# Second attention of a two-layer vision tower: the moving average's products and adds placed in its first iterations

## The chip, the cores and the metric

One core of a Trainium2 chip runs the whole program. The metric is device time in microseconds (us) of that core. TensorE, VectorE, ScalarE and GpSimd are called PE, DVE, ACT and POOL in the profile.

## What is computed

64 images become 65 tokens of 128 channels each; two layers follow, each with an attention and experts, and a normalisation after each of the four. The part that matters is the third normalisation's input: an attention and a moving average over the same `x`, blended by two weights.

```python
def _L1_attn_ref(x, ...):
    ...
    dots = jnp.einsum('bhid,bhjd->bhij', q, k) * dk ** (-0.5)
    ...
    dots = dots * mask.astype(dots.dtype)
    attn = jax.nn.softmax(dots, axis=-1)
    out_attn = jnp.einsum('bhij,bhjd->bhid', attn, v)
    out_attn = out_attn.transpose(0, 2, 1, 3).reshape(b, n, e) @ W_out + b_out
    def step(h, xt):
        h = p_coeff[None] * xt[:, :, None] + q_coeff[None] * h
        return (h, jnp.sum(gamma[None] * h, axis=-1))
    h0 = jnp.zeros((b, e, ndim), x.dtype)
    _, ys = jax.lax.scan(step, h0, jnp.swapaxes(x, 0, 1))
    x_cema = jnp.swapaxes(ys, 0, 1)
    w = jax.nn.softmax(adaptive_weights)
    return w[0] * out_attn + w[1] * x_cema

h = _L0_tok_ref(...)
h = _layernorm(h + _L0_attn_ref(h, ...), axis=-1)
h = _layernorm(h + _L0_ffn_ref(h, ...), axis=-1)
h = _layernorm(h + _L1_attn_ref(h, ...), axis=-1)
h = _layernorm(h + _L1_ffn_ref(h, ...), axis=-1)
```

## The kernel before, in words

Everything is float32. The 64 images are worked on in 16 groups of 4 (260 token columns). `vision_tower` (L1907) calls the stages one after the other; each is a block with one hand-written list per engine, and between two blocks all engines meet. In order: `embed_and_attend`, `route_and_gather`, `run_experts`, `scatter_and_norm`, `moving_average`, `attend_causally`, `norm_and_route`.

`scatter_and_norm` (L1127) adds the experts' outputs `yout` to the tokens and normalises; it leaves the result twice: by feature in `h_feat` (what projections read) and by token in `h_tok`. GpSimd puts `h_tok` plus a bias into `base`. A transfer on SyncE brings `lags` meanwhile: for each of the 128 channels a 65x65 matrix that turns the recurrence of the reference into one product over tokens.

`moving_average` (L1282) multiplies channel by channel: 16 chunks of 8 channels, each chunk filling one bank of 512 columns (64 images by 8 channels), four banks in turn. TensorE (L1302) signals `done` per chunk, VectorE (L1310) adds the bank, times the blend's weight, to `base` and signals `added`; TensorE needs `added` of four chunks back.

`attend_causally` (L1315) is a software pipeline over groups. `pipeline` (L97) runs an engine's loop with a lead: its variable g starts at -2 or -1, and one pass works on several groups, so that group g + 2 is projected and group g + 1 scored while group g is finished. The first and the last passes are written out; a hardware loop runs the middle. Per group:

- TensorE projects queries and keys (L1380, L1381) into the bank group `b_scores`. ScalarE copies queries into `qm` (L1558), which waits before its first pass for `v_cleared`, and keys into `kt` (L1561). GpSimd builds `qlast` for the last token (L1647) and copies the group's features to `b_h` (L1640).
- TensorE makes scores (L1372, L1375). VectorE masks them into `e` (L1478), finds the peaks and subtracts them (L1484 to L1497). ScalarE takes exponents (L1550), VectorE sums and inverts (L1503, L1505), GpSimd multiplies (L1655).
- TensorE makes values (L1386), ScalarE copies them to `vs` (L1582). TensorE turns the weights (L1400 to L1413), ScalarE copies them to `at` (L1570), TensorE multiplies by the values (L276), ScalarE copies to `ot`, TensorE applies the output weights (L1395), and VectorE adds `base` into `z` (L1513).

The scores of group g + 1 wait until the values of group g are out of `b_scores`. Before its first pass GpSimd clears `vs` twice and half of `at` (L1664, L1666); VectorE makes `parity_bias` (L1523) and, after a product with `mean` (L1432), `gate` (L1525); TensorE waits for that `gate` before its first pass.

## Time and profile before

| | |
|---|---|
| median of 3 runs | 704.71 us (704.68 to 706.1) |
| profiled execution | 712.94 us, its span 711.0 us |
| PE busy | 575.1 us, 81% |
| DVE busy | 489.5 us, 69% |
| ACT busy | 339.7 us, 48% |
| POOL busy | 249.3 us, 35% |

Busy time is that of the whole span. The stages differ in what limits them, so the page's shares say little about one of them; the stretch from 466 to 510 us, where `moving_average` ends in `attend_causally`, is read from the table of stretches (busy time and granted clock of an interval) and from the timelines of single engines. PE's clock is given as a share of its full speed: 1.00 is 2.4 GHz, 0.50 is 1.2 GHz.

### The profile page before, as it was taken

The numbers are of one execution on the slowest core, as the hardware profiler recorded it, in microseconds if no ns is written. First come the engines' busy times: TensorE is split into PE (matmuls) and PEld (weight loads), VectorE is DVE, ScalarE is ACT, GpSimd is POOL, SyncE is SP. The second block draws the span as 40 slices with busy tenths as digits, with TensorE's granted clock in tenths as the row PEclk, the third lists the DMA queues.
The fourth block names the chain that finished last, engine by engine and source line by source line (L and its number), as shares of the span: only waits on it lengthen the run. The fifth ranks groups of instructions, "written<-read, shape, count | busy, mean of one in ns | idle before, by whom it ended". The sixth has DMA issues, their size and how long they took to land. (4 is left out here: it accounts for less than half of the span.)

```text
span 711.0 us, 20891 instructions
## 1 busy us (share of the span) xinstructions
PE 575.1 (81%) x8467; PEld 478.8 (67%) x8467; DVE 489.5 (69%) x1011; ACT 339.7 (48%) x883; POOL 249.3 (35%) x251
## 2 busy tenths in 40 slices
PE   1999999999999999877479989786799999971013
PEld 0778888888888888766275378785677777761012
DVE  4166778888878788675444557755688888945883
ACT  0013444444444444335345368812678788855710
POOL 6253444444333333340102226622355555520001
PEclk9999999999999999968789999977799999975555
DMA  9444333333333359600260096000000000001210
GB/s 370 176 169 162 117 120 134 125 137 136 136 136 136 136 164 138 79 2 5 52 189 4 1 132 110 1 2 1 2 5 0 0 0 1 3 2 53 70 28 4
DMA packets 36104, 57.46 MB, mean 81 GB/s; under 512 B 19581, under 2 KB 33005, under 8 KB 33421
## 3 DMA queue, kind: packets, MB, share of 16 engines
q1 hardware_dynamic: 35952, 56.60, 28.2%
q8 instruction: 41, 0.67, 0.4%
q14 instruction: 15, 0.12, 0.1%
q0 software_dynamic: 96, 0.07, 0.0%
HBM read 50.12 MB, written 6.54 MB: 80 GB/s over the span
## 5 line engine op out<-in xcount | busy, mean ns | idle before, releaser
L406 PE MATMUL a_bank<-a_x,a_tok_w 128*128 128x256 f32 (+1 forms) x608 | 150.9, 391 | 16.0 <-DVE a_ht L702 16.0
L406 PEld LDWEIGHTS a_bank<-a_x,a_tok_w 128*128 128x128 f32 (+1 forms) x608 | 113.7, 193 | 37.7 <-issue 21.2
L828 POOL TENSOR_TENSOR a_qp<-a_cosine,a_swapped 128x260 f32<-128x260 f32 x16 | 15.1, 945 | 180.4 <-DVE a_swapped L614 180.4
L131 POOL TENSOR_TENSOR a_qt<-a_qp,data 128x512 f32<-128x512 f32 x64 | 73.3, 1176 | 2.1 <-POOL a_qp L828 1.7
L289 ACT ACTIVATE a_at<-a_bank 65x256 f32<-65x256 f32 x128 | 39.0, 391 | 25.3 <-PE a_bank L266 25.3
L1274 POOL TENSOR_TENSOR base<-h_tok,bias 65x512 f32<-65x512 f32 x16 | 30.2, 1892 | 38.6 <-ACT h_tok L1257 38.6
L1655 POOL TENSOR_TENSOR b_e<-b_e,b_inv 128x585 f32<-128x585 f32 (+1 forms) x32 | 35.5, 1110 | 23.3 <-DVE b_inv L1505 23.3
L266 PE MATMUL a_bank<-a_mix,a_e 64*65 64x64 f32 x1024 | 39.1, 229 | 1.7 <-ACT a_at L289 1.5
L202 ACT ACTIVATE a_e<-a_e 128x390 f32<-128x390 f32 (+1 forms) x48 | 24.1, 510 | 34.0 <-DVE a_e L182 34.0
L153 PE MATMUL a_bank<-a_kt,a_qt 128*64 128x65 f32 x1024 | 35.7, 230 | 5.0 <-issue 3.4
L179 DVE TENSOR_REDUCE a_mx<-a_bank 128x6 f32<-128x390 f32 (+1 forms) x48 | 25.7, 535 | 19.8 <-PE a_bank L153 19.4
L266 PEld LDWEIGHTS a_bank<-a_mix,a_e 64*65 64x65 f32 x1024 | 34.7, 142 | 5.8 <-issue 3.7
L153 PEld LDWEIGHTS a_bank<-a_kt,a_qt 128*64 128x64 f32 x1024 | 33.4, 144 | 7.7 <-issue 5.3
L1570 ACT ACTIVATE b_at<-b_bank 65x512 f32<-65x512 f32 x64 | 34.5, 591 | 7.3 <-PE b_bank L1413 7.2
L593 DVE SCALAR_TENSOR_TENSOR a_ht<-a_bank,data 128x256 f32<-128x256 f32 x16 | 7.7, 483 | 43.4 <-PE a_bank L406 43.4
L202 ACT ACT_TABLE_LOAD x14 | 18.0, 1283 | 39.9 <-DVE a_e L182 39.7
L1558 ACT ACTIVATE b_qm<-b_scores,b_parity_bias,tables 128x260 f32<-128x260 f32 x32 | 16.4, 564 | 34.4 <-POOL b_at L1666 25.0
L1171 PE MATMUL s_bank<-s_yrows,base 128*65 128x128 f32 x128 | 25.3, 279 | 4.8 <-ACT s_yrows L1239 4.8
L1833 PE MATMUL e_bank<-e_colsum,tables 65*65 65x8 f32 x16 | 3.1, 266 | 31.4 <-DVE e_colsum L1757 31.4
L1503 DVE TENSOR_REDUCE b_total<-b_e 128x9 f32<-128x585 f32 (+1 forms) x32 | 23.1, 721 | 7.7 <-ACT b_e L1550 7.7
L642 DVE RECIPROCAL a_rs<-a_sd 128x260 f32<-128x260 f32 x16 | 28.2, 1765 | 0.0
L1478 DVE TENSOR_TENSOR b_e<-b_scores,tables 128x520 f32<-128x520 f32 x32 | 20.8, 692 | 9.3 <-PE b_scores L1375 7.6
(283 smaller groups left out, 1473.7 us busy)
## 6 DMA issues: line engine op xcount, KB each, us to landing
a_x<-in_x SPq DMA_DIRECT2D x16, 2304.0 KB, 7.9
lag_rows<-a_kernel SPq DMA_DIRECT2D x1, 4192.5 KB, 40.3
lags<-lag_rows SPq DMA_DIRECT2D x1, 2112.5 KB
out<-e_plain SPq DMA_DIRECT2D x16, 130.0 KB
expert_weights<-in_w SPq DMA_DIRECT2D x2, 1024.0 KB, 13.8
lags<-lag_rows SPq DMA_DIRECT2D x1, 2047.5 KB
a_tok_w<-in_tok_w SPq DMA_DIRECT2D x1, 1152.0 KB, 6.4
base<-places SPq DMA_DIRECT2D x2, 520.0 KB
```

The costliest lines, as they stand in the source:

```text
L131: nc.gpsimd.tensor_tensor(qt[:, b * BLOCKS * P:(b + 1) * BLOCKS * P].rearrange("p (c h i) -> p c h i", i=qb, h=HEADS), wide(by_image[:, b, ...
L153: mm = nc.tensor.matmul(o[r * HALF:(r + 1) * HALF, :], qt[:, at_q:at_q + HALF], kt[:, b * TOKENS:(b + 1) * TOKENS], start=True, stop=True)
L179: nc.vector.tensor_reduce(mx[:, s0:s1], raw, AX.X, ALU.max).then_inc(S.max_done, 1)
L202: nc.scalar.activation(e[:, s0:s1, :], e[:, s0:s1, :], ACT.Exp, scale=HEAD ** -0.5).then_inc(S.exp_done, 1)
L266: mm = nc.tensor.matmul(mixbanks[r][0:TOKENS, col:col + HALF], e[rows, b * BLOCKS + c, :], mix[rows, :], start=True, stop=True)
L289: nc.scalar.activation(own[:, :, r], mixbanks[r][0:TOKENS, cols].rearrange("t (c h i) -> t c h i", c=BLOCKS, h=HEADS), ACT.Copy).then_inc( ...
L406: mm = nc.tensor.matmul(banks[0][:, 0:GP], w[0:rows, k * DIM:(k + 1) * DIM], x[p][0:rows, k * GP:(k + 1) * GP], start=(k == 0), stop=(k == ...
L642: nc.vector.reciprocal(rs[:, :], sd[:, :]).then_inc(S.inverse, 1)
L1171: nc.tensor.matmul(here, put(n, n + 1)[:, 0, b, :], rows[n % 2][:, b * DIM:(b + 1) * DIM], start=True, stop=False)
L1274: nc.gpsimd.tensor_tensor(R.base[0:TOKENS, n, :].rearrange("t (b d) -> t b d", b=GI), tok(n), wide(R.bias1[0:TOKENS, :].unsqueeze(1), [TOK ...
L1570: nc.scalar.activation(own, turnbanks[q][0:TOKENS, :].rearrange("t (b r i) -> t b r i", b=2, r=STRIPS), ACT.Copy).then_inc(S.at_ready, 1)
L1655: nc.gpsimd.tensor_tensor(e[:, part, :], e[:, part, :], wide(inv[:, part].unsqueeze(2), [P, size, TOKENS]), ALU.mult).then_inc(S.probs_rea ...
```

## The change

- `moving_average` goes away. Its products become `average(c0, c1)` in TensorE's list of `attend_causally`, its adds `add_average(c0, c1)` in VectorE's. They use the attention's own four banks `b_bank`, chunk c in bank c % 4, with the same rule for `added`.
- TensorE: in pass -2, behind group 0's queries and keys, it makes chunks 0 and 1, waits for the gate, and makes chunk 2. In pass -1 it makes chunks 3 to 5 behind group 0's scores, and 6 to 15 behind group 0's values; then it waits until all 16 are added. The wait for the gate ahead of the loop is gone.
- VectorE adds chunks 0 to 2 ahead of its loop, 3 to 7 between group 0's shifts and its first inversion, 8 to 15 behind the second inversion.
- GpSimd's clearing moves from ahead of the loop to the end of pass -2, behind `copy(0)`. ScalarE's wait for it moves from ahead of the loop to just before group 0's `save_values`.
- `vs`, `e`, `at`, `ot`, `z` and `sq` become pieces of the memory of `yout`, since `lags` now stays allocated.
- The first layer's semaphores are cleared ahead of `scatter_and_norm`'s block, not of the moving average's.

```diff
@@ -1134,6 +1134,7 @@
         banks = [ctx.enter_context(nc.psum_tensor(f"s_bank{i}", [P, 512], F32)) for i in range(6)]
         S = named_semaphores(R.ctx, nc, "s_", "turned rows_ready scattered summed centred "
                   "squared var_ready sd_ready inverse h_done tail_done feat_saved")
+        nc.clear_and_free_semaphores(list(R.first_layer))
...
-def moving_average(nc, A, R, lags):
-
-    with ExitStack() as ctx:
-        CH = 512 // IMAGES
-        CHUNKS = DIM // CH
-        banks = [ctx.enter_context(nc.psum_tensor(f"c_bank{i}", [P, 512], F32)) for i in range(4)]
-        S = named_semaphores(R.ctx, nc, "c_", "done added")
-        nc.clear_and_free_semaphores(list(R.first_layer))
-        tok = by_channel(R)
-        base = R.base[0:TOKENS, :, :].rearrange("t g (b d) -> t (g b) d", b=GI)
-        block = ctx.enter_context(nc.Block())
-
-        @block.tensor
-        def _(pe):
-            pe.wait_ge(R.lags_in, 32)
-            for c in range(CHUNKS):
-                bank = banks[c % 4][0:TOKENS, :].rearrange("t (b e) -> t b e", e=CH)
-
-                wait_past(pe, S.added, c - 3)
-                for j in range(CH):
-                    mm = nc.tensor.matmul(bank[:, :, j], lags[:, c * CH + j, :], tok[:, c * CH + j, :], start=True, stop=True)
-                mm.then_inc(S.done, 1)
-
-        @block.vector
-        def _(dve):
-            for c in range(CHUNKS):
-                dve.wait_ge(S.done, c + 1)
-                here = base[:, :, c * CH:(c + 1) * CH]
-                nc.vector.scalar_tensor_tensor(
-                    out=here, in0=banks[c % 4][0:TOKENS, :].rearrange("t (b e) -> t b e", e=CH),
-                    scalar=R.blend[0:TOKENS, 1:2], in1=here, op0=ALU.mult, op1=ALU.add).then_inc(S.added, 1)
-
-
-def attend_causally(nc, A, R):
+def attend_causally(nc, A, R, lags, spare):
...
+        CH = 512 // IMAGES
+        CHUNKS = DIM // CH
+        home = [0]
+
+        def reuse(n):
+            home[0] += n
+            return spare[:, home[0] - n:home[0]]
...
-        vs = [sb(f"vs{i}", [P, PADDED]) for i in range(2)]
-        e = [sb(f"e{i}", [P, SLOTS, TOKENS]) for i in range(2)]
+        vs = [reuse(PADDED) for i in range(2)]
+        e = [reuse(SLOTS * TOKENS).rearrange("p (s t) -> p s t", s=SLOTS) for i in range(2)]
         mx, total, inv = sb("mx", [P, SLOTS]), sb("total", [P, SLOTS]), sb("inv", [P, SLOTS])
-        at = sb("at", [P, GI, HEADS, TOKENS])
-        ot = sb("ot", [P, GT])
-        z, sq = sb("z", [TOKENS, GI, DIM]), sb("sq", [TOKENS, GI, DIM])
+        at = reuse(GI * HEADS * TOKENS).rearrange("p (b h t) -> p b h t", b=GI, h=HEADS)
+        ot = reuse(GT)
+        z, sq = (reuse(GI * DIM)[0:TOKENS].rearrange("t (b d) -> t b d", b=GI) for i in range(2))
...
+        by_image = R.base[0:TOKENS, :, :].rearrange("t g (b d) -> t (g b) d", b=GI)
+        tok = by_channel(R)
...
+            def average(c0, c1):
+                for c in range(c0, c1):
+                    bank = banks[c % 4][0:TOKENS, :].rearrange("t (b e) -> t b e", e=CH)
+
+                    wait_past(pe, S.added, c - 3)
+                    for j in range(CH):
+                        mm = nc.tensor.matmul(bank[:, :, j], lags[:, c * CH + j, :], tok[:, c * CH + j, :], start=True, stop=True)
+                    mm.then_inc(S.averaged, 1)
+
             nc.tensor.matmul(banks[2][:, 0:EXPERTS1], T("mean"), D("gate1"), start=True, stop=True).then_inc(S.gate_mean, 1)
-            pe.wait_ge(S.gate_ready, 1)
             for g, i, p in pipeline(pe, 2, GROUPS + 2):
                 if exists(g + 1):
                     scores(g + 1)
+                if isinstance(g, int) and g == -1:
+                    average(3, 6)
                 if exists(g - 2):
                     turn_rows(g - 2)
                 if exists(g):
@@ -1451,10 +1439,18 @@
 
                         pe.wait_ge(S.masked, 2 * (g + 2))
                     queries_keys(g + 2)
+                if isinstance(g, int) and g == -2:
+                    pe.wait_ge(R.lags_in, 32)
+                    average(0, 2)
+                    pe.wait_ge(S.gate_ready, 1)
+                    average(2, 3)
                 if exists(g + 1):
 
                     pe.wait_ge(S.masked, 2 * (g + 2))
                     values(g + 1, 1 - p)
+                if isinstance(g, int) and g == -1:
+                    average(6, CHUNKS)
+                    pe.wait_ge(S.added, CHUNKS)
...
+            def add_average(c0, c1):
+                for c in range(c0, c1):
+                    dve.wait_ge(S.averaged, c + 1)
+                    here = by_image[:, :, c * CH:(c + 1) * CH]
+                    nc.vector.scalar_tensor_tensor(
+                        out=here, in0=banks[c % 4][0:TOKENS, :].rearrange("t (b e) -> t b e", e=CH),
+                        scalar=R.blend[0:TOKENS, 1:2], in1=here, op0=ALU.mult, op1=ALU.add).then_inc(S.added, 1)
+
+            add_average(0, 3)
             for g, i, p in pipeline(dve, 1, GROUPS + 1):
                 if exists(g + 1):
                     dve.wait_ge(S.scores_done, g + 2)
@@ -1536,12 +1542,17 @@
                     shift_last(g + 1, e[1 - p])
                     peaks(g + 1, 1, e[1 - p])
                     shift(g + 1, 1, e[1 - p])
+                    if isinstance(g, int) and g == -1:
+                        add_average(3, 8)
                     invert(g + 1, 0, e[1 - p])
                 if exists(g - 1):
                     residual(g - 1)
                     total_of_rows(g - 1)
                 if exists(g + 1):
                     invert(g + 1, 1, e[1 - p])
+                if isinstance(g, int) and g == -1:
+                    add_average(8, CHUNKS)
+                    dve.wait_ge(S.added, CHUNKS)
...
-            act.wait_ge(S.v_cleared, 3)
             act.wait_ge(S.biased, 1)
             for g, i, p in pipeline(act, 2, GROUPS + 2):
                 if exists(g - 2):
@@ -1624,6 +1634,8 @@
                     save_pair(g, 1)
                 if exists(g + 1):
                     exponent(g + 1, 1, e[1 - p])
+                    if isinstance(g, int) and g == -1:
+                        act.wait_ge(S.v_cleared, 3)
                     save_values(g + 1, 1 - p)
...
-            for i in range(2):
-                nc.gpsimd.memset(vs[i][:, :], 0.0).then_inc(S.v_cleared, 1)
-            pool.wait_ge(S.v_cleared, 2)
-            nc.gpsimd.memset(at[HALF:, :, :, :], 0.0).then_inc(S.v_cleared, 1)
-            pool.wait_ge(S.v_cleared, 3)
+            def clear():
+                for i in range(2):
+                    nc.gpsimd.memset(vs[i][:, :], 0.0).then_inc(S.v_cleared, 1)
+                pool.wait_ge(S.v_cleared, 2)
+                nc.gpsimd.memset(at[HALF:, :, :, :], 0.0).then_inc(S.v_cleared, 1)
+                pool.wait_ge(S.v_cleared, 3)
+
             for g, i, p in pipeline(pool, 2, GROUPS + 1):
                 if exists(g + 2):
                     last_queries(g + 2)
@@ -1676,6 +1690,8 @@
                     normalise(g + 1, 1, e[1 - p])
                 if exists(g + 2):
                     copy(g + 2, p)
+                if isinstance(g, int) and g == -2:
+                    clear()
...
-            moving_average(nc, A, R, lags)
+            attend_causally(nc, A, R, lags, yout[:, :, :, :].rearrange("p g b s -> p (g b s)"))
         yout_home.close()
-        attend_causally(nc, A, R)
```

TensorE, the end of `scatter_and_norm` (s_) to the first turned weights of `attend_causally` (b_); c_ is the moving average. Before:

```order
L1182 MATMUL s_bank<-tables,h_tok 128x65 x16
L1130 UNCONDITIONAL_BRANCH
L1294 UNCONDITIONAL_BRANCH
L1302 MATMUL c_bank<-h_tok,lags 65x64 x128
L1284 UNCONDITIONAL_BRANCH
L1358 UNCONDITIONAL_BRANCH
L1432 MATMUL b_bank<-data,tables 128x8
L1380 MATMUL b_scores<-h_feat,data 128x260
L1381 MATMUL b_scores<-h_feat,data 128x260
L1372 MATMUL b_scores<-b_kt,b_qm 64x65 x32
```

And with the change:

```order
L1419 MATMUL b_bank<-data,tables 128x8
L1358 MATMUL b_scores<-h_feat,data 128x260
L1359 MATMUL b_scores<-h_feat,data 128x260
L1416 MATMUL b_bank<-h_tok,lags 65x64 x24
L1350 MATMUL b_scores<-b_kt,b_qm 64x65 x32
L1353 MATMUL b_scores<-b_kt,b_qlast 32x65 x4
L1416 MATMUL b_bank<-h_tok,lags 65x64 x24
L1358 MATMUL b_scores<-h_feat,data 128x260
L1359 MATMUL b_scores<-h_feat,data 128x260
L1364 MATMUL b_scores<-data,b_h_0 65x128 x4
L1416 MATMUL b_bank<-h_tok,lags 65x64 x80
L1350 MATMUL b_scores<-b_kt,b_qm 64x65 x32
```

The 128 products stand now as 24, 24 and 80 between the projections, scores and values of group 0 and those of group 1, and one pair of branches (a block's end and start) is gone.

VectorE with the change, from the block's start to group 1's mask; `yout` is the name under which the order prints all tiles in that memory, here `e`:

```order
L1519 TENSOR_SCALAR b_parity_bias<-tables,data 128x2
L1521 TENSOR_TENSOR b_gate<-data,b_bank 128x8
L1527 SCALAR_TENSOR_TENSOR base<-b_bank,blend,base 65x64x8 x3
L1474 TENSOR_TENSOR yout<-b_scores,tables 128x520 x2
...
L1485 TENSOR_TENSOR yout<-yout,b_mx 128x520
L1527 SCALAR_TENSOR_TENSOR base<-b_bank,blend,base 65x64x8 x5
L1499 TENSOR_REDUCE b_total<-yout 128x9
L1501 RECIPROCAL b_inv<-b_total 128x9
L1499 TENSOR_REDUCE b_total<-yout 128x8
L1501 RECIPROCAL b_inv<-b_total 128x8
L1527 SCALAR_TENSOR_TENSOR base<-b_bank,blend,base 65x64x8 x8
L1474 TENSOR_TENSOR yout<-b_scores,tables 128x520 x2
```

The 16 adds, which stood in one row behind each other ahead of the parity product, are split 3, 5 and 8.

## Rows read from the trace of the kernel before

**Rows 1.** Stretches: from:to, us, busy us (count) of PE, PEld, DVE, ACT, POOL, PEclk, DMA.
```profile
466.50:472.20 5.70, 5.64 (x53) 5.67 (x54) 1.59 (x3) 0.00 (x0) 0.00 (x0) 0.52 0.00 0
472.20:485.50 13.30, 12.21 (x207) 12.09 (x206) 10.37 (x14) 0.00 (x0) 0.02 (x1) 1.00 0.01 2
...
491.00:500.00 9.00, 5.47 (x84) 4.25 (x84) 5.24 (x11) 4.38 (x7) 1.11 (x3) 0.50 0.01 2
500.00:506.50 6.50, 6.40 (x102) 5.30 (x102) 4.81 (x11) 3.17 (x7) 3.29 (x4) 0.53 0.01 3
```

**Rows 2.** Timeline of TensorE: start, us, engine, line, operation, tiles, count, [idle before, releaser].
```profile
466.56 17.85 PE L1302 MATMUL c_bank<-h_tok,lags 128*65 128x64 f32 x256 [1.38 <-PEq L1130]
...
485.52 0.36 PE L1432 MATMUL b_bank<-data,tables 128*128 128x8 f32 x2 [1.10 <-PEq L1284]
...
491.07 1.29 PE L1372 MATMUL b_scores<-b_kt,b_qm 32*64 32x65 f32 x64 [2.50 <-POOL b_qlast L1647]
...
494.17 1.23 PE L1380 MATMUL b_scores<-h_feat,data 128*128 128x260 f32 x2 [1.43 <-DVE b_e L1478]
...
495.19 1.07 PE L1381 MATMUL b_scores<-h_feat,data 128*128 128x260 f32 x2
...
500.10 1.29 PE L1372 MATMUL b_scores<-b_kt,b_qm 32*64 32x65 f32 x64 [2.13 <-ACT b_vs L1582]
...
509.71 0.91 PE L1372 MATMUL b_scores<-b_kt,b_qm 32*64 32x65 f32 x64 [0.54 <-ACT b_vs L1582]
...
510.54 0.32 PE L1375 MATMUL b_scores<-b_kt,b_qlast 128*32 128x65 f32 x8
...
512.29 0.70 PE L1380 MATMUL b_scores<-h_feat,data 128*128 128x260 f32 x2 [0.50 <-DVE b_e L1478]
...
513.27 1.04 PE L1386 MATMUL b_scores<-data,b_h 128*65 128x128 f32 x8
...
517.25 0.91 PE L1372 MATMUL b_scores<-b_kt,b_qm 32*64 32x65 f32 x64
```

**Rows 3.** Timeline of VectorE, moving average and the block after it.
```profile
468.59 0.75 DVE L1310 SCALAR_TENSOR_TENSOR base<-c_bank,blend,base 65x512 f32<-65x512 f32 x1 [2.95 <-PE c_bank L1302]
...
470.35 0.75 DVE L1310 SCALAR_TENSOR_TENSOR base<-c_bank,blend,base 65x512 f32<-65x512 f32 x1 [1.01 <-PE c_bank L1302]
...
473.09 0.75 DVE L1310 SCALAR_TENSOR_TENSOR base<-c_bank,blend,base 65x512 f32<-65x512 f32 x1 [0.23 <-PE c_bank L1302]
...
484.45 0.75 DVE L1310 SCALAR_TENSOR_TENSOR base<-c_bank,blend,base 65x512 f32<-65x512 f32 x1 [0.20 <-PE c_bank L1302]
...
485.52 1.83 DVE L1523 TENSOR_SCALAR b_parity_bias<-tables,data 128x2 f32<-128x2 f32 x1 [0.32 <-PEq L1284]
...
492.80 1.31 DVE L1478 TENSOR_TENSOR b_e<-b_scores,tables 128x520 f32<-128x520 f32 x2 [5.45 <-PE b_scores L1375]
...
496.28 0.70 DVE L1489 TENSOR_TENSOR b_e<-b_e,b_mx 128x520 f32<-128x520 f32 x1
...
498.87 0.77 DVE L1503 TENSOR_REDUCE b_total<-b_e 128x9 f32<-128x585 f32 x1 [1.89 <-ACT b_e L1550]
...
500.47 0.20 DVE L1505 RECIPROCAL b_inv<-b_total 128x8 f32<-128x8 f32 x1
```

**Rows 4.** Timeline of ScalarE, first groups of the second attention.
```profile
489.25 1.03 ACT L1558 ACTIVATE b_qm<-b_scores,b_parity_bias,tables 128x260 f32<-128x260 f32 x2 [24.97 <-POOL b_at L1666]
...
496.85 1.28 ACT L1550 ACT_TABLE_LOAD   x1
...
498.14 1.22 ACT L1550 ACTIVATE b_e<-b_e 128x585 f32<-128x585 f32 x2
```

**Rows 5.** Timeline of GpSimd, start of the second attention.
```profile
485.48 1.85 POOL L1664 MEMSET b_vs<- 128x1024 f32 x2 [19.25 <-POOLq L1284]
...
487.39 1.83 POOL L1666 MEMSET b_at<- 64x2080 f32 x1
...
490.42 0.50 POOL L1647 TENSOR_TENSOR b_qlast<-b_qm,tables 128x128 f32<-128x128 f32 x1 [1.21 <-ACT b_qm L1558]
```

More of the change, by code:

```diff
@@ L1327, in attend_causally @@
         banks = [ctx.enter_context(nc.psum_tensor(f"b_bank{i}", [P, 512], F32)) for i in range(4)]
-        S = named_semaphores(R.ctx, nc, "b_", "scores_done masked max_done shifted exp_done summed inverted probs_ready "
+        S = named_semaphores(R.ctx, nc, "b_", "averaged added scores_done masked max_done shifted exp_done summed inverted probs_ready "
                              "turned at_ready av_done ot_ready y_done z_ready sum_done mean_scaled centred squared "
```

## Prediction

> **What bounds the kernel now.** I read the table of stretches first, then the timelines of the engines around the moving average and the first two groups of the second attention. All times below are on the trace's axis, or "+x", meaning x us after 466.56, where the moving average's first product starts.
>
> From 466.56 to 485.2 the kernel does one thing: TensorE multiplies 16 chunks of the moving average and VectorE adds each one to `base`. TensorE is nearly always busy, VectorE works 12 of 19 us, ScalarE and GpSimd do nothing [rows 1]. The first 5.6 us run at the lower of TensorE's two levels (granted 0.52, which is 1.2 GHz), the rest at 2.4 GHz. A chunk takes 1.76 us at the lower level (468.59 to 470.35) and 0.947 us at the upper (473.09 to 484.45 is 12 chunks) [rows 3]. So here the bound is TensorE.
>
> From 485.52, when the next block begins, it is the other way round: a chain of small steps hands group 0 from engine to engine and TensorE mostly waits. ScalarE copies the queries of group 0 only at 489.25, released by GpSimd's memset of `at` [rows 4], the last of three, which ends at 487.39 + 1.83 = 489.22 [rows 5]. Then GpSimd's last queries, scores at 491.07 [rows 2], VectorE's mask, peaks and shift from 492.80 to 496.98 [rows 3], exponents, values, and at 500.10 the scores of group 1 [rows 2]. I call 485.52 to 500.10 the *fill*; it lasts 14.58 us. In 491 to 500 TensorE has 5.47 of 9 us of work and its clock is granted at 0.50; it is still 0.53 in 500 to 506.5, though TensorE is then busy for 6.40 of 6.5 us [rows 1]. Group 1's scores to group 2's therefore take 509.71 - 500.10 = 9.61 us, where the next iteration, at the upper level, takes 517.25 - 509.71 = 7.54 us [rows 2].
>
> From the moving average's start to group 1's scores is 500.10 - 466.56 = 33.54 us. The change lays the two parts of it over each other. Everything before 466.56 and everything after 509.71 issues the same instructions on the same engines.
>
> **The change, step by step.** TensorE's new list, in its order:
>
> - Gate mean, 0.36 [rows 2]: +0.4.
> - Queries and keys of group 0 at the lower level, 494.17 to 496.26, 2.09 [rows 2]: +2.5. They no longer wait for the gate's subtraction.
> - Chunks 0 and 1 at 1.76, the clock rising at +5.6 as it does now: +5.8. Chunk 2 at the upper level, 0.95: +6.75.
> - Scores of group 0, 509.71 to 510.86 in a row at the upper level, 1.15 [rows 2]: +7.9. What they need is there: ScalarE's two query copies take 1.03 from about +1.6 [rows 4], and GpSimd's last queries 0.50 behind them [rows 5], so by about +3.2.
> - Chunks 3 to 5, 2.85: +10.75.
> - Queries and keys of group 1 and values of group 0, 512.29 to 514.31, 2.02 [rows 2]: +12.8.
> - Chunks 6 to 15, ten times 0.947: +22.3. VectorE's last add, 0.75 [rows 3], and two hand-overs of about 0.1: **+23.3**.
>
> VectorE's list: its mask starts at about +8.0, and mask to shift takes 496.98 - 492.80 = 4.18 [rows 3]: +12.2. Five adds (chunks 3 to 7) at 0.75: +15.95. ScalarE's table load of 1.28 and its two exponents, 1.22, come after the copies of group 1 [rows 4], from about +13.1, so they are done at about +15.7, and the two inversions run without a wait, 498.87 to 500.67, 1.80 [rows 3]: +17.75. Eight adds at 0.75: **+23.75**. The lists touch only loosely: chunk 12 may start when chunk 8 is added, at +18.5, and TensorE wants it at +18.5. Back-to-back adds of different banks may be closer than 0.75, the two masks of 0.70 each fit into 1.31 [rows 3]. I take +23.5, between the two ends.
>
> So group 1's scores start at 466.56 + 23.5 = 490.1 instead of 500.10: **10.0 us**. What lies beside other work here: VectorE's 12 us of adds under TensorE's products, and the whole chain of group 0 under the products too. What is on the path is TensorE's own work.
>
> - *Group 1's iteration.* TensorE comes to it at the upper level, so I give it the 7.54 of the next one instead of 9.61: **2.1 us**. The softmax of group 0 is ready long before (its inversions end at +17.75, and GpSimd's two products follow them at once).
> - *Clearing moved.* The memsets follow the copy of group 0's features on GpSimd, from about +3.9, and take 1.85 + 1.83 = 3.7 [rows 5]: done at +7.6. What waits behind them on GpSimd is group 1's last queries, which need a copy that ScalarE makes at about +12.7; ScalarE's own wait stands now before the values of group 0, near +13. Cost nothing; without that cover ScalarE would wait at most until +7.6.
> - *Buffers shared.* The tiles have other addresses; the only wait this could need, for the experts' outputs being read, is over before the block. Nothing.
> - *One block fewer, semaphores cleared one block earlier.* From VectorE's last add, 484.45 + 0.75, to the next block is 0.32 [rows 3]; that is inside the 33.54. The boundary at 466.56 stays. The clear is one instruction on GpSimd, which has nothing to do at the start of the scatter block. Nothing, and at worst that 0.3.
>
> Sum: 10.0 + 2.1 = 12.1 us. The profiled execution took 712.94 us with a span of 711.0; that would become 700.8. It is 1.2% above the median of 704.71, so I take the 12.1 from the median: **692.6 us**.
>
> **Two unknown prices.** First, whether memsets hold VectorE. The tiny parity product of 128x2 starts at 485.52 and takes 1.83 us [rows 3]; it ends at 487.35, GpSimd's first two memsets at 485.48 + 1.85 = 487.33 [rows 5]. It looks held. In the changed kernel the adds of chunks 0 to 2 fall beside the memsets. If those are held too, they run from +7.6 to +9.85, the mask starts 1.85 later, and so does the end. The other bound is nothing. I take nothing, since the add is not of that product's form (it reads a bank). The Trainium skill, "SBUF — State Buffer", section "Who interferes with whom", says that a one-input product between SBUF tiles can take a lock shared with GpSimd, and that an operation with at most one SBUF input outside such modes takes none; by it the parity product is held, which the row bears out, and the adds are not, so its sum is 692.6 and not 694.5. No row before shows an add beside a memset.
>
> Second, when the clock rises. A chunk at the lower level costs 1.76 - 0.95 = 0.81 more, so 1 us spent at that level costs 0.46. If it were up from the start, 5.6 x 0.46 = 2.6 us less: 690.0. If it took as long as from 491 to 506.5 now, 15.5 us, it would be 4.6 more: 697.2. I take 5.6, the value for the same products with the same idle time before them. The Trainium skill, "TensorE: Matmul & The Clock Gate", section "What's actually happening", says that the number of slow products at a start differs between runs of one kernel; that bears on the width, not on the middle.
>
> **The rivals.**
>
> - *A, forecast, 0.70:* 692.6 us.
> - *B, VectorE is held by the memsets or becomes the bound, 0.12:* 12.1 - 1.9 = 10.2 saved, 694.5 us. For it speaks the row of the parity product, and that VectorE's list is as long as TensorE's; against it, the add's form.
> - *C, the clock rises late, 0.09:* for it, that queries, keys and scores with their short hand-overs now stand between the products, and that the clock stayed low from 491 to 506.5; against it, that TensorE has no wait over 0.2 us in its list until +22. 697.2 us.
> - *D, little is hidden, 0.02:* two engines wait for each other at each bank and the chain of group 0 is still exposed; only the 3.7 us of memsets and the boundary's 0.3 go: about 701 us.
> - *E, slower, 0.05:* the clock does not rise at all before group 1's scores. Then TensorE's list is 0.36 + 2.09 + 16 x 1.76 + 1.73 (scores, 491.07 to the mask at 492.80) + 2.02 x 1.86 + 0.95 = 37.0 us against 33.54, and group 1's iteration stays at 9.61: 3.5 us slower, 708.2 us. It decides from about 32 us at the lower level on (12.1 / 0.46 = 26 beyond 5.6). A rise between about 29 and 35 us would land within 0.2% of before, 0.02. Against both: the clock rose 5.6 us into the same products.
>
> About 0.2% (1.4 us) is what a measurement of this kernel can tell from no change. A to D are faster by more than that, 0.93 together; the rise near 32 us is the 0.02 within it, and E is the 0.05 slower. The range holds A, B and C with the bounds of both unknown prices, 690.0 to 697.5 us, and leaves out D and E.
>
> **What would show it.** In the changed profile: about 0.3 us between blocks at 466.5 and none at 485; the clock rising some 5 to 7 us in; scores of group 0 ending near +8; group 1's scores near 490.1 and group 2's 7.5 us later; adds of 0.75 with none stretched; GpSimd's memsets from +4 to +8 with nobody released by them. I am wrong if TensorE's row is broken by waits for `added`, if an add beside a memset lasts 1 us or more, if the first 6 chunks all take 1.76, or if group 1's iteration still lasts 9 us or more.

## The result, and the profile after

| | before | with the change |
|---|---|---|
| median | 704.77 us (4 runs, 704.68 to 706.1) | 696.79 us (4 runs, 694.82 to 697.27) |
| profiled execution | 712.94 us, span 711.0 | 697.12 us, span 695.0 |

The ratio is 0.9861, 95% interval 0.9819 to 0.9902: faster by 1.0 to 1.8%. It is not the quotient of the two medians, which is 0.9887. Forecast were 692.6 us (690.0 to 697.5) and a gain of 12.1 us; the medians moved by 8.0 us, the ratio stands for 9.8. The time lies in the range, at its upper end.

First the timeline of TensorE with the change; L1419 is the gate's mean, with which the block starts, so "+x" counts now from 462.34.

```profile
462.34 0.57 PE L1419 MATMUL b_bank<-data,tables 128*128 128x8 f32 x2 [1.36 <-PEq L1130]
462.76 1.21 PE L1358 MATMUL b_scores<-h_feat,data 128*128 128x260 f32 x2
463.76 1.07 PE L1359 MATMUL b_scores<-h_feat,data 128*128 128x260 f32 x2
464.63 4.80 PE L1416 MATMUL b_bank<-h_tok,lags 128*65 128x64 f32 x48
469.36 0.92 PE L1350 MATMUL b_scores<-b_kt,b_qm 32*64 32x65 f32 x64
470.21 0.32 PE L1353 MATMUL b_scores<-b_kt,b_qlast 128*32 128x65 f32 x8
470.46 3.05 PE L1416 MATMUL b_bank<-h_tok,lags 128*65 128x64 f32 x48
...
474.28 1.04 PE L1364 MATMUL b_scores<-data,b_h 128*65 128x128 f32 x8
475.16 9.62 PE L1416 MATMUL b_bank<-h_tok,lags 128*65 128x64 f32 x160
485.62 0.92 PE L1350 MATMUL b_scores<-b_kt,b_qm 32*64 32x65 f32 x64 [0.84 <-DVE base L1527]
...
493.36 0.91 PE L1350 MATMUL b_scores<-b_kt,b_qm 32*64 32x65 f32 x64 [0.54 <-ACT yout L1593]
```

These rows answer to [rows 2]. The second block of the section is gone, and TensorE goes from the gate's mean to chunk 15 (475.16 + 9.62 = 484.78) without an idle time that the row would show in brackets. Group 1's scores start at 485.62, which is +23.28, where they stood 33.54 us after the moving average's first product; group 2's follow 7.74 us later instead of 9.61. The stretch up to group 2's scores, which I call the *section*, takes 493.36 - 462.34 = 31.02 us against 43.15: 12.1 us less.

VectorE and GpSimd in the same stretch, against [rows 3, 5]:

```profile
462.34 0.23 DVE L1519 TENSOR_SCALAR b_parity_bias<-tables,data 128x2 f32<-128x2 f32 x1 [0.90 <-PEq L1130]
462.94 0.16 DVE L1521 TENSOR_TENSOR b_gate<-data,b_bank 128x8 f32<-128x8 f32 x1 [0.37 <-PE b_bank L1419]
466.63 0.75 DVE L1527 SCALAR_TENSOR_TENSOR base<-b_bank,blend,base 65x512 f32<-65x512 f32 x1 [3.53 <-PE b_bank L1416]
468.39 0.75 DVE L1527 SCALAR_TENSOR_TENSOR base<-b_bank,blend,base 65x512 f32<-65x512 f32 x1 [1.01 <-PE b_bank L1416]
469.47 0.75 DVE L1527 SCALAR_TENSOR_TENSOR base<-b_bank,blend,base 65x512 f32<-65x512 f32 x1 [0.34 <-PE b_bank L1416]
470.60 1.31 DVE L1474 TENSOR_TENSOR yout<-b_scores,tables 128x520 f32<-128x520 f32 x2 [0.38 <-PE b_scores L1353]
...
474.69 3.37 DVE L1527 SCALAR_TENSOR_TENSOR base<-b_bank,blend,base 65x512 f32<-65x512 f32 x5
...
479.69 3.99 DVE L1527 SCALAR_TENSOR_TENSOR base<-b_bank,blend,base 65x512 f32<-65x512 f32 x6
...
484.82 0.75 DVE L1527 SCALAR_TENSOR_TENSOR base<-b_bank,blend,base 65x512 f32<-65x512 f32 x1 [0.20 <-PE b_bank L1416]
```

```profile
465.95 1.85 POOL L1677 MEMSET yout<- 128x1024 f32 x2
467.86 1.83 POOL L1679 MEMSET yout<- 64x2080 f32 x1
475.21 0.50 POOL L1659 TENSOR_TENSOR b_qlast<-b_qm,tables 128x128 f32<-128x128 f32 x1 [5.53 <-ACT b_qm L1569]
```

The memsets run from 465.95 to 469.69. The adds at 466.63 and 468.39 stand inside that and last 0.75 like all others; nobody waits for the memsets. The parity product, which took 1.83, takes 0.23 now, and the gate's subtraction behind it 0.16 (in the kernel before it started at 485.92 and took 1.44). VectorE's last adds wait 0.20 for their chunk, so it is TensorE that sets the end.

The table of stretches (columns as in [rows 1]): the block's first 5.5 us, then the rest up to group 1's scores.

```profile
462.30:467.80 5.50, 5.46 (x35) 5.00 (x36) 1.14 (x3) 1.39 (x3) 2.63 (x4) 0.50 0.00 0
467.80:485.60 17.80, 16.98 (x314) 16.44 (x312) 15.97 (x27) 4.38 (x7) 4.85 (x5) 0.98 0.01 3
```

The clock is at half for these 5.5 us and, by the 0.98 of the next 17.8, for about 0.7 us more, so for about 6.2 us in all; VectorE's rows show it too, the second add 1.76 us behind the first, the third only 1.08 behind the second. From then on it is full. At the moving average's start it had been half for about 5.5 us (0.52 over 5.7 us [rows 1]). Before, it fell again inside the fill (0.50 from 491 to 500).

So the section did what the forecast said. The question is why the medians moved by less than 12.1.

### The profile page after: what moved, and what is told of

Read it like the earlier page. It is cut to its first block and busy times, and to the rows that moved or that the text cites. A ratio compares the mean times of both kernels' runs of the same rounds, so it can differ in the third digit from the quotient of the medians.

```text
span 695.0 us, 20882 instructions
## 1 busy us (share of the span) xinstructions
PE 568.2 (82%) x8467; PEld 473.3 (68%) x8467; DVE 486.5 (70%) x1011; ACT 339.5 (49%) x883; POOL 249.2 (36%) x251
## 5 line engine op out<-in xcount | busy, mean ns | idle before, releaser
L1667 POOL TENSOR_TENSOR yout<-yout,b_inv 128x585 f32<-128x585 f32 (+1 forms) x32 | 35.5, 1110 | 22.7 <-DVE b_inv L1501 22.7
L1581 ACT ACTIVATE yout<-b_bank 65x512 f32<-65x512 f32 x64 | 34.4, 590 | 12.3 <-PE b_bank L1391 12.2
L593 DVE SCALAR_TENSOR_TENSOR a_ht<-a_bank,data 128x256 f32<-128x256 f32 x16 | 7.7, 484 | 43.4 <-PE a_bank L406 43.4
L153 PE MATMUL a_bank<-a_kt,a_qt 128*64 128x65 f32 x1024 | 34.3, 227 | 2.8 <-issue 1.2
L1659 POOL TENSOR_TENSOR b_qlast<-b_qm,tables 128x128 f32<-128x128 f32 x16 | 13.7, 858 | 40.0 <-ACT b_qm L1569 40.0
L182 DVE TENSOR_TENSOR a_e<-a_bank,a_mx 128x390 f32<-128x390 f32 (+1 forms) x48 | 26.0, 542 | 1.6
L1672 POOL TENSOR_TENSOR base<-yout,b_means 65x512 f32 (+1 forms) x16 | 16.6, 1036 | 28.2 <-ACT b_means L1600 28.2
```

Of the source, the lines that this page charges most:

```text
L153: mm = nc.tensor.matmul(o[r * HALF:(r + 1) * HALF, :], qt[:, at_q:at_q + HALF], kt[:, b * TOKENS:(b + 1) * TOKENS], start=True, stop=True)
L182: nc.vector.tensor_tensor(part, raw, wide(mx[:, s0:s1].unsqueeze(2), [P, n, TOKENS]), ALU.subtract).then_inc(S.shifted, 1)
L1581: nc.scalar.activation(own, turnbanks[q][0:TOKENS, :].rearrange("t (b r i) -> t b r i", b=2, r=STRIPS), ACT.Copy).then_inc(S.at_ready, 1)
L1667: nc.gpsimd.tensor_tensor(e[:, part, :], e[:, part, :], wide(inv[:, part].unsqueeze(2), [P, size, TOKENS]), ALU.mult).then_inc(S.probs_rea ...
```

## The experiments

Two theories were put up. Theory 1: the section is worth 12 us, and what is missing lies elsewhere, above all in differences between executions of the same kernel. Theory 2: in ordinary executions the section of the kernel before is shorter than in the profiled one. Eleven kernels ran, three of them repeats without an edit, in three sets; each set had its own runs of the kernel before (medians 708.03 of 23 runs, 705.96 of 17, 706.79 of 11).

**1. The kernel before, again** (no edit).

> The kernel before once more, for a profile of an ordinary execution (704.7 us; the profiled one took 712.94). Theory 1, the section is as profiled and the missing 4 us lie elsewhere: from the moving average's first product to the scores of group 2 it takes 43.2 us again, and the 8 us that 712.94 was too long lie in other stages, such as the last groups of the first layer, where TensorE's clock fell from 305 to 320. Theory 2, the section itself differs between executions: it takes about 39 us in an ordinary one, so that the change can save only 8 there. Time 704.7 us by both.

Measured: median 706.28 us (10 runs, 700.21 to 709.29), ratio 0.9998 (0.9959 to 1.0038). Its TensorE rows:

```profile
460.98 18.03 PE L1302 MATMUL c_bank<-h_tok,lags 128*65 128x64 f32 x256 [1.38 <-PEq L1130]
480.11 0.36 PE L1432 MATMUL b_bank<-data,tables 128*128 128x8 f32 x2 [1.10 <-PEq L1284]
...
494.68 1.29 PE L1372 MATMUL b_scores<-b_kt,b_qm 32*64 32x65 f32 x64 [2.12 <-ACT b_vs L1582]
504.40 0.91 PE L1372 MATMUL b_scores<-b_kt,b_qm 32*64 32x65 f32 x64 [0.54 <-ACT b_vs L1582]
```

The section is 504.40 - 460.98 = 43.42 us, as in the first profile, and it starts 5.6 us earlier. From its start to the end of the span it is 705.2 - 460.98 = 244.2 us, against 711.0 - 466.56 = 244.4. The difference between the two profiles lies ahead of the section. It goes with the clock: among these ten executions those with a mean granted clock of 0.898 and 0.901 took 708.5 and 709.3 us, those with 0.912 and 0.913 took 700.2 to 703.2. Theory 1, for this execution. The spread of one kernel, 9 us in these ten (11.5 us in the other 23 of the set, 700.27 to 711.79), is as large as the effect.

**2. The changed kernel, again** (no edit), in the first and in the third set.

> The changed kernel once more, timed in five rounds. Both theories: about 696.8 us, the section 31.0 us. Theory 1: the time before the section's start varies between executions (462.34 in the profile), more than 1 us. Theory 2: it does not.

> The changed kernel again, as the measure for the next two on the same chip: 695 to 698 us, 9 to 12 us below the kernel before; the section 31 us.

Measured: 697.37 us (6 runs, 693.79 to 698.37), ratio 0.9887 (0.9839 to 0.9934); and 697.23 us (6 runs, 694.67 to 701.81), ratio 0.9875 (0.983 to 0.992). The sections are 30.71 and 30.98 us; they start at 463.42 and 462.20, against 462.34 in the first profile, just over the 1 us apart that theory 1 named; experiment 4 has one at 457.23. So the first pair of medians had the kernel before from the lower part of its spread: against the sets' own medians the change gives 10.7 and 9.6 us, and the ratios stand for 8.0 and 8.8 us.

**3. Merged, but nothing laid over.** All chunks and adds stand ahead of the first pass; the calls inside the passes go.

```diff
+            pe.wait_ge(R.lags_in, 32)
+            average(0, 2)
+            pe.wait_ge(S.gate_ready, 1)
+            average(2, CHUNKS)
+            pe.wait_ge(S.added, CHUNKS)
             for g, i, p in pipeline(pe, 2, GROUPS + 2):
...
-            add_average(0, 3)
+            add_average(0, CHUNKS)
+            dve.wait_ge(S.added, CHUNKS)
```

> The changed kernel, but all 16 chunks and their adds ahead of the attention's first pass: blocks merged and clearing moved, nothing laid over. If the overlap is what saves: 0.4 + 17.9 for products, then a fill without the wait for the memsets and for the gate, about 12, so group 1's scores 30 us after the block's start (33.5 before, 23.3 in the changed kernel), and group 1's iteration still at the lower clock level, 9.6 us. That is 3.5 saved against the kernel before, so some 8 to 9 us slower than the changed kernel. Rival, the merged block and the cleared memsets are what saves and the overlap only moves work: within 2 us of the changed kernel.

```profile
462.06 0.57 PE L1419 MATMUL b_bank<-data,tables 128*128 128x8 f32 x2 [1.38 <-PEq L1130]
462.48 18.18 PE L1416 MATMUL b_bank<-h_tok,lags 128*65 128x64 f32 x256
...
484.05 0.90 PE L1350 MATMUL b_scores<-b_kt,b_qm 32*64 32x65 f32 x64 [1.42 <-POOL b_qlast L1650]
...
492.64 1.29 PE L1350 MATMUL b_scores<-b_kt,b_qm 32*64 32x65 f32 x64 [2.13 <-ACT yout L1584]
502.57 0.90 PE L1350 MATMUL b_scores<-b_kt,b_qm 32*64 32x65 f32 x64 [0.54 <-ACT yout L1584]
```

Measured: 703.93 us (10 runs, 699.51 to 705.74), ratio 0.996 (0.9922 to 0.9998). Group 1's scores start 30.58 us after the block, 30 were expected, and the iteration takes 9.93, at half clock again. The section is 40.51 us: merging and clearing alone give 2.6 of the 12.1 us, the overlap 9.5. A part of these 9.5 is the clock: group 1's iteration takes 9.93 here and 7.74 with the overlap, 2.2 us. The medians put it 6.6 us behind the changed kernel of its set, less than the 8 to 9 expected; part of it, 1.3 us of the drain, shows in experiment 7.

**4. The clearing ahead again.**

```diff
+            clear()
             for g, i, p in pipeline(pool, 2, GROUPS + 1):
...
+            act.wait_ge(S.v_cleared, 3)
             act.wait_ge(S.biased, 1)
```

> The changed kernel with the clearing and ScalarE's wait for it ahead of the loops again. By my steps: ScalarE copies queries at +3.8, GpSimd's last queries end at +5.4, still ahead of chunk 2's end at +7, so no time; the parity product lasts 1.8 us again, and adds lose nothing. Rival, the cover is too thin: scores of group 0 start after +8 and the kernel is 1 us or more slower.

VectorE, GpSimd and ScalarE at the block's start:

```profile
457.23 1.83 DVE L1519 TENSOR_SCALAR b_parity_bias<-tables,data 128x2 f32<-128x2 f32 x1 [0.91 <-PEq L1130]
```
```profile
457.19 1.85 POOL L1676 MEMSET yout<- 128x1024 f32 x2 [0.29 <-POOLq L1130]
```
```profile
460.96 1.03 ACT L1569 ACTIVATE b_qm<-b_scores,b_parity_bias,tables 128x260 f32<-128x260 f32 x2 [6.00 <-POOL yout L1678]
```

Measured: 696.24 us (5 runs, 691.93 to 696.53), ratio 0.988 (0.982 to 0.994). The section is 488.07 - 457.23 = 30.84 us, between the changed kernel's 30.71 and 31.02. ScalarE copies at +3.7 as expected, and chunk 2 covers it. In the changed kernel the clearing's place is worth nothing. What it would be worth without the products beside it no run shows alone; experiment 3 has it together with the merged block. And the parity product is held again: it ends at 459.06, the first memsets at 457.19 + 1.85 = 459.04.

**5. TensorE kept busy at the end of the scatter block.** Ten products into a seventh bank, where TensorE waits in the last passes: 4 in pass 15, 2 in each of passes 16 and 17, and 2 behind the loop. The expectation says 12; the edit and the trace have 10.

```diff
+            def busy(n):
+                for _ in range(n):
+                    nc.tensor.matmul(banks[6][:, 0:256], T("ident"), R.data[:, 0:256], start=True, stop=True)
...
+                if g >= GROUPS - 1:
+                    busy(4 if g == GROUPS - 1 else 2)
                 if inside(g - 2):
                     tail(g - 2)
+            busy(2)
```

> The changed kernel with 12 products of 256 columns, whose result nobody reads, where TensorE waits in the last passes of the scatter block. If the section's first 5 us lack only the clock: chunks 0 and 1 take 0.95 instead of 1.76, all of the section is 2.2 to 2.6 us shorter (group 1's scores 20.7 to 21.1 us after the block's start instead of 23.3), the kernel 2 to 2.6 us faster than the changed one, since VectorE's list (20.9) still fits. Rival: VectorE or the hand-overs bind as soon as TensorE is quicker, and less than 1 us is left; or the extra products delay the last turns of the scatter block by as much as they give.

The stretches just before and at the block's start, here and then in the changed kernel just before it:

```profile
456.00:460.10 4.10, 3.43 (x16) 2.53 (x16) 1.04 (x3) 1.60 (x6) 3.75 (x3) 1.00 0.00 0
460.10:466.00 5.90, 5.86 (x137) 5.49 (x138) 3.15 (x6) 1.39 (x3) 3.70 (x5) 1.00 0.01 3
```
```profile
458.30:462.30 4.00, 1.70 (x8) 1.32 (x8) 1.04 (x3) 1.51 (x6) 3.65 (x3) 0.50 0.00 0
```

TensorE's timeline with the ten products:

```profile
460.14 0.36 PE L1426 MATMUL b_bank<-data,tables 128*128 128x8 f32 x2 [0.52 <-PEq L1130]
...
461.32 3.00 PE L1423 MATMUL b_bank<-h_tok,lags 128*65 128x64 f32 x48
...
480.50 0.92 PE L1357 MATMUL b_scores<-b_kt,b_qm 32*64 32x65 f32 x64 [0.84 <-DVE base L1534]
488.27 0.91 PE L1357 MATMUL b_scores<-b_kt,b_qm 32*64 32x65 f32 x64 [0.57 <-ACT yout L1600]
```

Measured: 694.41 us (6 runs, 690.99 to 698.92), ratio 0.9844 (0.98 to 0.9888). The clock stays at full, chunks 0 to 2 take 3.00 instead of 4.80, group 1's scores start at +20.36 and the section takes 28.13 us: 2.9 us less, where 2.2 to 2.6 were expected. That fits the 6.2 us at half clock read above, at the prediction's 0.46 us each. The scatter block itself keeps its length (401.52 to 460.14, 58.6 us, as in the others). Not all of the gain arrives at the end: from the section's start to the span's end it is 230.9 us against 232.7, 1.8 less, because the drain (experiment 7) took 28.5 us here and 27.5 there. The set had no run of the changed kernel without extra products, and the interval overlaps that kernel's in the other sets, so the section shows the gain, not the medians.

**6. TensorE kept busy at the end of the first layer**, in the kernel before, in the changed one, and in the changed one with the ten products of experiment 5.

```diff
+            def busy(n, bank=0):
+                for _ in range(n):
+                    nc.tensor.matmul(banks[bank][:, 264:440], T("ident"), R.data[:, 0:176], start=True, stop=True)
...
+                    elif last(g):
+                        pe.wait_ge(S.ht_ready, GROUPS)
+                        busy((2, 2, 5, 3, 0)[n])
...
+            busy(4, 4)
             var(n - 1, 2)
...
+            busy(1, 4)
             mean(n, 0)
+            busy(2, 4)
             var(n, 0)
+            busy(2, 4)
             pe.wait_ge(S.tok_saved, n - 1)
             tail(n - 1)
+            busy(6, 4)
```

> The kernel before with products that nobody reads in the last passes of the first layer, where the trace shows TensorE's clock at half and where executions of one kernel differ. If those differences come from the clock there, the time from the start to the scatter block's end is 457 to 461 us in the profile, 1 to 5 less than in most, and the executions lie closer together. Rival: the spread has another source (transfers), then nothing changes; or the extra products themselves cost 2 to 4 us.

> The changed kernel with the same extra products in the first layer. Against the kernel before with them, medians 11 to 12 us apart if the change is worth what the section shows (33.5 + 9.6 against 23.3 + 7.7). Rival: 8 us apart, if something outside the section is slower because of the change.

> The changed kernel with both sets of extra products. If they add up: 2 to 2.6 us below the changed kernel with the first set alone, and the fastest of all.

Measured in one set: 703.85 us (12 runs, 701.44 to 706.5), ratio 0.9967 (0.9939 to 0.9996); 692.49 us (7 runs, 691.4 to 697.07), ratio 0.9808 (0.9773 to 0.9844); 691.04 us (6 runs, 689.46 to 693.39), ratio 0.9798 (0.9762 to 0.9835).

With the same extra products in both, the medians are 703.85 - 692.49 = 11.4 us apart, as expected by theory 1; by the spread of the single runs I estimate that this is known to about 2 us. The two profiles don't say the same: their sections are 41.0 - 30.6 = 10.4 us apart and, because the drain is longer with the change (experiment 7), the stretches from the section's start to the span's end only 242.0 - 233.1 = 8.9. So the rival of the second expectation, that something outside the section is slower, is not refuted.

The kernel before gains 2 us from the extra products and its spread falls from 7.7 us (17 runs) to 5.1 (12 runs), as expected. Its section starts at 457.49, inside the 457 to 461 expected, but that of the changed kernel at 461.93, so one profile doesn't settle where it starts. With the second set of products in addition the median is another 1.5 us lower, where 2 to 2.6 were expected; by the profiles it is 2.7 (233.1 and 230.4 from the section's start to the end).

The profile of the kernel before with them also shows theory 2's case, a shorter section. The stretches of the moving average's start, of the fill from group 0's scores on, and TensorE's rows:

```profile
457.50:462.50 5.00, 5.00 (x63) 5.00 (x64) 2.12 (x3) 0.00 (x0) 0.00 (x0) 0.71 0.01 3
480.70:489.80 9.10, 5.47 (x84) 4.26 (x85) 5.32 (x11) 4.38 (x7) 1.21 (x3) 0.62 0.01 2
```
```profile
475.24 0.36 PE L1444 MATMUL b_bank<-data,tables 128*128 128x8 f32 x2 [1.11 <-PEq L1296]
...
489.82 0.91 PE L1384 MATMUL b_scores<-b_kt,b_qm 32*64 32x65 f32 x64 [2.13 <-ACT b_vs L1594]
498.49 0.91 PE L1384 MATMUL b_scores<-b_kt,b_qm 32*64 32x65 f32 x64 [0.54 <-ACT b_vs L1594]
```

The section is 498.49 - 457.49 = 41.0 us, 2.2 to 2.4 less than in the other two profiles, at two places. At the moving average's start the clock was at half for only about 2.9 us (0.71 over 5.0 us), and the stretch up to the next block takes 475.24 - 457.49 = 17.75 us instead of 18.96: 1.2 us. And it came up inside the fill, so that group 1's scores last 0.91, not 1.29, and the iteration 8.67, not 9.61: 0.9 us. The fill itself keeps its 14.58 us. Against such an execution the change saves 10 us in the section, not 12. This kernel has the extra products, though; both profiles of the kernel before without them have the long section, so that its ordinary executions have the short one is not shown.

**7. Where the rest of a microsecond is.** No further kernel: after the loop's last scores, the groups drain. From group 15's scores to the next block's first VectorE instruction it takes 27.2 and 26.7 us in the two profiles of the kernel before, 26.9 with the extra products of experiment 6, 26.7 with merged blocks, but 27.5, 28.0 and 27.5 in the three of the changed kernel. The stretches from 12 us after group 15's scores, changed kernel first, then before (experiment 1):

```profile
615.00:619.00 4.00, 4.00 (x80) 3.34 (x77) 0.95 (x2) 1.08 (x2) 0.00 (x0) 0.57 0.01 4
619.00:623.00 4.00, 1.47 (x15) 1.27 (x15) 0.48 (x1) 2.10 (x12) 1.03 (x1) 0.89 0.00 0
```
```profile
626.00:630.00 4.00, 2.87 (x83) 2.23 (x78) 1.43 (x2) 1.74 (x6) 0.38 (x1) 1.00 0.01 4
630.00:634.00 4.00, 2.32 (x14) 2.25 (x15) 0.00 (x0) 1.45 (x10) 0.66 (x1) 0.58 0.00 0
```

The same work, 12 us into the drain, ran at half clock in the one (0.57) and at full in the other. Why the clock falls earlier there was not tried; that it is the earlier fall that costs the time follows from the rows, not from an experiment. Nor does it belong to the changed kernel alone: in the first profile of the kernel before the clock fell about 13 us into the drain (0.79 from 631.3 to 633.3, then 0.50), and that is the drain of 27.2. Nor to the overlap as such: the variants of the changed kernel in experiments 4 to 6 drained in 27.8 to 28.5 us, those of experiment 8 in 26.7 and 26.5.

**8. The wait for the last add behind group 1's scores.**

```diff
                     average(6, CHUNKS)
-                    pe.wait_ge(S.added, CHUNKS)
...
                     average(3, 6)
+                if isinstance(g, int) and g == 0:
+                    pe.wait_ge(S.added, CHUNKS)
```

> The changed kernel, but TensorE waits for the last add only behind the scores of group 1, ahead of the turns that need the adds' banks. In the changed kernel TensorE sits idle for 0.84 us there, and VectorE needs the scores next. If that hand-over is on the path, the scores of group 2 start 0.8 us earlier (30.2 us after the block's start) and the kernel gains 0.8 us, less than the medians can tell. Rival: VectorE's list is the longer one, then nothing.

> The changed kernel with both sets of extra products and the late wait: section 27.3 us (31.0 - 2.9 - 0.8), median 4 to 7 us below the changed kernel, about 690 us. Rival: with the clock up from the start the chain of VectorE binds, and the section stays at 28.1 us as with both sets of extra products.

TensorE's timeline with the late wait alone, then with all three edits:

```profile
461.08 0.57 PE L1419 MATMUL b_bank<-data,tables 128*128 128x8 f32 x2 [1.38 <-PEq L1130]
...
483.65 0.91 PE L1350 MATMUL b_scores<-b_kt,b_qm 32*64 32x65 f32 x64
491.39 0.91 PE L1350 MATMUL b_scores<-b_kt,b_qm 32*64 32x65 f32 x64 [0.54 <-ACT yout L1594]
```
```profile
458.94 0.36 PE L1438 MATMUL b_bank<-data,tables 128*128 128x8 f32 x2 [0.52 <-PEq L1142]
...
478.39 0.92 PE L1369 MATMUL b_scores<-b_kt,b_qm 32*64 32x65 f32 x64
486.13 0.91 PE L1369 MATMUL b_scores<-b_kt,b_qm 32*64 32x65 f32 x64 [0.54 <-ACT yout L1613]
```

Measured: 695.56 us (6 runs, 692.73 to 698.34), ratio 0.9841 (0.98 to 0.9882), for the late wait alone; the idle 0.84 us are gone from the row and the section is 30.31 us, 0.4 to 0.7 less. From group 0's scores to group 1's it is 483.65 - 468.30 = 15.35 us instead of 16.26, so the edit gives the 0.8 expected and a little more; the section shows less of it because in this profile the clock stayed at half for about 6.6 us, longer than in the others. To the span's end it is 1.6 us less (231.1 against 232.7), but 0.8 of that is the shorter drain, which nothing here ties to the edit. With all three edits: 689.37 us (6 runs, 687.01 to 692.85), ratio 0.9762 (0.9719 to 0.9804), section 27.19 us, where 27.3 were expected. Its interval lies below that of the changed kernel of the same set (0.983 to 0.992): it beats both kernels, 7.9 us below the changed one.

All profiles side by side, in us:

| kernel | block start | group 1's scores | group 2's | section start to span's end |
|---|---|---|---|---|
| before | 466.56 | +33.5 | +43.2 | 244.4 |
| before, again | 460.98 | +33.7 | +43.4 | 244.2 |
| before, busy first layer | 457.49 | +32.3 | +41.0 | 242.0 |
| merged only | 462.06 | +30.6 | +40.5 | 241.3 |
| changed | 462.34 | +23.3 | +31.0 | 232.7 |
| changed, again | 463.42 | +23.0 | +30.7 | 232.9 |
| changed, third time | 462.20 | +23.2 | +31.0 | 232.6 |
| clearing first | 457.23 | +23.1 | +30.8 | 232.8 |
| changed, busy first layer | 461.93 | +22.9 | +30.6 | 233.1 |
| busy end of scatter | 460.14 | +20.4 | +28.1 | 230.9 |
| both busy | 456.99 | +20.4 | +28.1 | 230.4 |
| late wait | 461.08 | +22.6 | +30.3 | 231.1 |
| all three | 458.94 | +19.5 | +27.2 | 227.9 |

The last column takes out what happens ahead of the section; it orders the kernels far better than the medians, whose spreads overlap.

## Why the prediction was right, and where its size was off

- **The section.** Forecast 10.0 us up to group 1's scores and 2.1 for the iteration. Measured in the pair of profiles: 33.54 - 23.28 = 10.3 and 9.61 - 7.74 = 1.9. The mechanism, TensorE as the bound with the chain of group 0 under its products, holds, and experiment 3 shows that the overlap carries it.
- **TensorE's list.** Forecast was +2.5 for the end of the keys, +6.75 for the start of group 0's scores, +10.75 for the end of chunk 5, +22.3 for that of chunk 15, +23.5 for group 1's scores; measured +2.5, +7.0, +11.2, +22.4, +23.3. That the end fits to the tenth is in part luck: chunk 5 ends 0.4 late, with the clock at half for 0.6 us longer than assumed, and the next step, forecast at 2.02, took 475.16 - 473.51 = 1.65.
- **VectorE's list.** I had its adds 0.75 apart and the list as long as TensorE's. Five adds take 3.37, so they follow each other every 0.66 us, and VectorE waits at the end. Experiment 5 shows the room: with TensorE 2.9 us quicker, group 1's scores still come 2.9 us earlier.
- **The memsets (rival B).** Refuted: adds beside them last 0.75. That a parity product between SBUF tiles is held is shown by experiment 4: 1.83 us beside the memsets, 0.23 without, with nothing else of its own changed. The Trainium skill, "SBUF — State Buffer", section "Who interferes with whom", has both halves of it, the lock for the one form and none for an operation with at most one SBUF input outside such modes; the runs agree (1.83 against 0.23 for the product, 0.75 for every add).
- **The clock (rival C).** It was at half for 5.5 to 6.2 us in the three profiles of the changed kernel, where 5.6 was forecast. Rivals D and E are refuted by group 1's scores at +23.3.
- **Where the size was off** is the last step of the sum: "It is 1.2% above the median of 704.71, so I take the 12.1 from the median". Three things bear on it. First, the base: 704.71 was the median of three runs, and the sets that followed have 705.96 to 708.03 for the same kernel; 12.1 below these is 693.9 to 695.9, not 692.6, so I estimate that 1.3 to 3.3 us of the missing 4.2 lie there. Second, "Everything before 466.56 and everything after 509.71 issues the same instructions on the same engines" holds, but the time is not the same: the drain took 0.3 to 1.3 us longer, with its clock falling earlier. Third, the section before need not always be 43.2: it was 43.4 in the second profile and 41.0 in the one with extra products. The third would take 0 to 2.2 us from the 12.1, the second 0.3 to 1.3, which leaves 8.6 to 11.8 us. The ratios of three comparisons (0.9861, 0.9887, 0.9875) stand for 8.0 to 9.8 us, the medians with extra products in both kernels for 11.4. Where in this band the change lies is open: each interval is some 6 us wide, and the profiles are too few to tell how often the section is shorter. Why the clock falls earlier in the drain is open too.
- **The size of a measurable difference.** I took 0.2% for what a measurement can tell, from three runs that happened to agree. Executions of this kernel lie 9 us apart and more (1.3%), and the intervals with six runs reach about 3 us to either side. The measured 696.8 lies 0.7 us inside the range, and the two repeats of the changed kernel have 697.4 and 697.2; with such a spread, that it lies inside is luck in part.

## What to carry to other kernels

When one stage is bound by one engine and the next is a chain that leaves this engine idle, write the list of the bound engine with the chain's short steps in it and add up its durations: the sum is the new length as long as every other engine's list is shorter, and it came out here within 0.3 us at the end, with 0.4 in between. The idle engine's clock belongs into that sum twice, since filling the gaps also keeps the clock up for what follows. Before taking a gain from a profile to a median, profile the same kernel twice and count from the changed place to the end: a profiled execution is one draw of a spread that can be as wide as the gain.

## What the runs showed of the hardware

- Executions of one kernel differed by 9 us (700.2 to 709.3), in step with the mean granted clock (0.898 to 0.913). By the profiles the places were the first layer (in the two of the kernel before, the routing block starts at 351.85 and 346.39), the routing (26.1 to 28.5 us from there to the experts without extra products) and the drain (26.5 to 28.5). The scatter block took 58.6 us in every profile. How much of the difference the clock makes at each place was not shown; extra products in the first layer took about 2 us off the kernel before.
- Ten products that nobody reads, put where TensorE waits, kept the clock at 1.00 over a boundary between blocks and saved 2.9 us in the section behind it, with the block ahead as long as before (58.6 us). To the span's end 1.8 us were left; the drain took 28.5 us, where it had taken 27.5.
- A product of 128x2 elements between SBUF tiles took 1.83 us, to the end of two GpSimd memsets behind each other (1.85 us), and 0.23 without them; the next VectorE instruction behind it took 1.44 instead of 0.16.
